# Mixture-of-experts kernel on one core: gathers signalled in halves, rows turned in the first and third round, constants' products in the turns without an expert

## What is computed

```python
def balanced_assignment(scores):
    T, E = scores.shape
    C = T // E
    taken = jnp.zeros((T,), dtype=bool)
    parts = []
    for e in range(E):
        s = jnp.where(taken, -jnp.inf, scores[:, e])
        _, idx = jax.lax.top_k(s, C)
        parts.append(idx)
        taken = taken.at[idx].set(True)
    return jnp.concatenate(parts)
...
norm = layer_norm(feat, ln_g, ln_b)
scores = jax.lax.stop_gradient(norm @ centroids.T)
sort_by_expert = balanced_assignment(scores)
routed = feat[sort_by_expert].reshape(E, C, D)
h = layer_norm(routed, ln_g, ln_b)
h = jax.nn.gelu(jnp.einsum('ecd,edf->ecf', h, w1) + b1[:, None, :])
h = jnp.einsum('ecf,efd->ecd', h, w2) + b2[:, None, :]
out = routed + h
```

## Time and profile before

| what | value |
|---|---|
| median of three runs | 1326.44 us (1326.17 to 1327.94) |
| the profiled execution's own time | 1329.28 us |
| its span in the profile | 1326.4 us |
| PE busy | 1122.2 us, 85% |
| DVE busy | 878.6 us, 66% |
| POOL busy | 775.3 us, 58% |
| ACT busy | 677.6 us, 51% |
| mean granted TensorE clock | 0.914 of full speed |

### The profile page before, as it was taken

One profiled execution on the slowest core, in us unless ns is written; L12 is line 12 of the kernel. 1 busy time (PEld: TensorE's weight loads), 2 busy tenths in 40 slices (PEclk: granted clock), 3 DMA queues, 4 the chain that ended last, 5 costly groups with the idle time before them and its releaser, 6 DMA issues. The chain is left out here.

```text
span 1326.4 us, 34010 instructions
## 1 busy us (share of the span) xinstructions
PE 1122.2 (85%) x11612; PEld 734.3 (55%) x11612; DVE 878.6 (66%) x2747; ACT 677.6 (51%) x1452; POOL 775.3 (58%) x829
## 2 busy tenths in 40 slices
PE   4999999999999996647998994869999635999996
PEld 1444444444444443434776773759998324677674
DVE  7677777777777775777788602765556768777720
ACT  3777766777776764401433453575555400343353
POOL 2878887877888785102555674645554102466675
PEclk8999999999999998856999997879999755999998
DMA  8000000000000000410221223200000410122221
GB/s 193 2 1 0 0 0 0 0 0 0 0 0 0 0 1 2 144 33 21 60 58 56 79 72 95 59 1 0 0 0 0 135 42 19 47 61 61 61 84 40
DMA packets 55851, 47.32 MB, mean 36 GB/s; under 512 B 13142, under 2 KB 47190, under 8 KB 55772
## 3 DMA queue, kind: packets, MB, share of 16 engines
q1 hardware_dynamic: 44748, 27.92, 7.6%
q0 software_dynamic: 8192, 17.84, 4.8%
q10 hardware_dynamic: 2832, 0.54, 0.3%
HBM read 28.44 MB, written 17.83 MB: 35 GB/s over the span
## 5 line engine op out<-in xcount | busy, mean ns | idle before, releaser
L349 POOL TENSOR_TENSOR patt_aa<-patt_aa,causal_aa 128x512 f32<-128x512 f32 x256 | 319.3, 1274 | 73.4 <-DVE patt_aa L528 71.5
L528 DVE TENSOR_TENSOR patt_aa<-p_second_aa,first_aa 128x512 f32<-128x512 f32 x384 | 247.5, 686 | 133.9 <-ACT first_aa L424 130.5
L424 ACT ACTIVATE first_aa<-p_first_aa 128x512 f32<-128x512 f32 x384 | 208.6, 596 | 135.9 <-PE p_first_aa L627 132.1
L627 PE MATMUL p_second_aa<-q_t_aa,k_t_aa 32*128 32x512 f32 x768 | 234.8, 641 | 0.0
L627 PE MATMUL p_first_aa<-q_t_aa,k_t_aa 32*128 32x512 f32 x768 | 217.1, 641 | 15.1 <-ACT first_aa L424 14.8
L1423 POOL DMA_INDIRECT rows_e<-norm_rows,index_e x128 | 124.5, 973 | 163.7 <-DVE index_e L1119 126.5
L646 PEld LDWEIGHTS p_z_aa<-patt_aa,v_aa 128*32 128x32 f32 x3072 | 72.2, 109 | 147.5 <-issue 79.6
L1386 ACT ACTIVATE hid_e<-p_h_e,b_e 128x512 f32<-128x512 f32 x128 | 88.6, 692 | 116.3 <-PE p_h_e L1255 116.3
L1255 PE MATMUL p_h_e<-rows_t_e,w_e 128*128 128x512 f32 x256 | 144.5, 675 | 0.1
L1340 PE MATMUL p_cnt_e<-reach_e,ones_e 128*128 128x120 bf16 x896 | 84.6, 250 | 69.7 <-DVE reach_e L1183 69.5
L1376 ACT ACTIVATE rows_t_e<-p_t_e,bias,gain 128x512 f32<-128x512 f32 x32 | 24.9, 779 | 210.7 <-PE p_t_e L1246 210.7
(11 more groups left out here) (260 smaller groups left out, 2065.4 us busy)
## 6 DMA issues: line engine op xcount, KB each, us to landing
norm_rows<-norm_n SPq DMA_DIRECT2D x32, 288.0 KB, 2.8
w_e<-L_ffn_w SPq DMA_DIRECT2D x32, 256.0 KB
x<-L_attn_a_x SPq DMA_DIRECT2D x8, 512.0 KB, 5.4
x<-ffn_rows SPq DMA_DIRECT2D x7, 512.0 KB, 6.8
rows_e<-norm_rows,index_e POOLq DMA_INDIRECT x128, 2.6
ffn_rows<-yb_e,index_e POOLq DMA_INDIRECT x64
out<-yb_e,index_e POOLq DMA_INDIRECT x64
x<-ffn_rows SPq DMA_DIRECT2D x2, 256.0 KB, 3.2
```

Source lines behind the costliest of these rows:

```text
L349: pool.tensor_tensor(patt[n % LAG][:, b, :, :], patt[n % LAG][:, b, :, :], causal[:, None, :].broadcast_to([P, 4, P]), ALU.mult).then_inc( ...
L424: act.activation(first[n % 2][:, b, :], p_first[b][:], ACT.Identity).then_inc(first_copied, 1)
L528: dve.tensor_tensor(patt[n % LAG][:, b, :, :].rearrange("p h q -> p (h q)"), p_second[(2 * n + b) % ROOMS][:], first[n % 2][:, b, :], ALU. ...
L627: pe.matmul(out[:], k_t[par][rows, half, keys * P:(keys + 1) * P], q_t[par][rows, half, :, queries * P:(queries + 1) * P], start=True, sto ...
```

## The change

It touches only `experts`, in five places.

- Each of the semaphores `gathered` becomes two, one for the gathered blocks 0 to 3 and one for 4 to 7, and `turn_rows(h)` waits for its own half only.
- TensorE's `pieces` are dealt out anew: the first turning stands in the first round behind three late downs, the second in the third round, the ups begin in the second round, and down 4 stays in its own turn.
- ScalarE copies the second half of the rows after gelu 2 and no longer ahead of gelu 0.
- VectorE's `add_back` stands at the head of window 0 (first half) and in window 2 (second half) instead of windows 2 and 4.
- In turns 0 and 1 each count is followed by three products of constants, `ones` by a 512 wide piece of `sixteenth`, into `p_h[0]`, which nobody reads.

```diff
-        gathered = [sem(f"gathered{i}_{tag}") for i in range(2)]
+        gathered = [[sem(f"gathered_{h}_{i}_{tag}") for i in range(2)] for h in range(2)]
...
                     if e >= 3:
-                        windows[2].append(lambda: add_back(e - 3, 0))
-                        windows[4].append(lambda: add_back(e - 3, 1))
+                        windows[0].insert(0, lambda: add_back(e - 3, 0))
+                        windows[2].append(lambda: add_back(e - 3, 1))
...
                     def turn_rows(h):
                         if h == 0:
-                            pe.wait_ge(gathered[par], 16 * SLOTS * half)
                             pe.wait_ge(wl[par], 48 * half)
+                        pe.wait_ge(gathered[h][par], 16 * SLOTS // 2 * half)
...
-                    late = [lambda t=t: down(t, c - 1, 1 - par) for t in range(4, SLOTS)] if rest else []
+                    late = [lambda t=t: down(t, c - 1, 1 - par) for t in range(5, SLOTS)] if rest else []
                     if compute:
-                        pieces = [late[0:2], late[2:4], turned, ups[0:1], ups[1:2], ups[2:4], ups[4:6], ups[6:8], downs[0:2], downs[2:4]]
+                        pieces = [late + turned[0:1], ups[0:2], ups[2:4] + turned[1:2], ups[4:5], ups[5:6], ups[6:7], ups[7:8] + downs[0:1],
+                                  downs[1:3], downs[3:4], downs[4:5]]
                     if isinstance(e, int) and e >= E:
-                        pieces[0:3] = [late[0:1], turned[0:1] + late[1:2], turned[1:2] + late[2:4]]
+                        pieces[0] = late[0:1] + turned[0:1] + late[1:2] + turned[1:2] + late[2:3]
+                        pieces[2] = ups[2:4]
                     if isinstance(e, int) and e == E + 1:
-                        pieces.append(downs[4:8])
+                        pieces.append(downs[5:8])
...
                         mm.then_inc(counted, 1)
+                        if not compute:
+                            for _ in range(3):
+                                pe.matmul(p_h[0][:], ones[:], sixteenth[:, 0:SLOTS, :].rearrange("p s t -> p (s t)"), start=True, stop=True)
                         for piece in pieces[n]:
                             piece()
...
-                    for h in range(2):
-                        copy_rows(h)
-                    for m in range(8):
+                    copy_rows(0)
+                    for m in range(3):
+                        gelu(m)
+                    copy_rows(1)
+                    for m in range(3, 8):
                         gelu(m)
...
                         pool.indirect_dma_start(rows[lpar][:, j, :], None, norm_rows,
-                                                bass.IndirectOffsetOnAxis(ap=list_of(l, lpar)[:, j:j + 1], axis=0)).then_inc(gathered[lpar], 16)
+                                                bass.IndirectOffsetOnAxis(ap=list_of(l, lpar)[:, j:j + 1], axis=0)).then_inc(gathered[j // 4][lpar], 16)
```

More of the change, by code:

```diff
@@ L1323, in turn @@
                                 rank_chosen(E - 1, (E - 1) % 2)
-                            if lists and n == 14:
+                            if lists and n == 13:
                                 for q in range(CHUNKS // 2):
                                     list_chunk(E - 1, q)
-                            if lists and n == 16:
+                            if lists and n == 15:
                                 list_fold(E - 1)
@@ L1334, in turn @@
                             pieces[n] = pieces[n] + [lambda q=q: list_chunk(l, q) for q in chunks]
-                        pieces[5] = pieces[5][0:1] + [lambda: list_fold(l)] + pieces[5][1:]
+                        pieces[5] = [lambda: list_fold(l)] + pieces[5]
                     for n in range(PASSES):
```

## The result

The changed kernel takes **1310.73 us** (median of 4 runs, 1309.76 to 1311.53), the kernel before 1326.62 beside it: a ratio of 0.9874, 95% interval 0.9862 to 0.9886. The forecast was 1310.6 in a range of 1304 to 1319. The profiled span is 1309.7 us, 16.7 less than before. The sum is right, but not every term of it is: one brought nothing, three others are too small, and one is a little too large.

What follows compares the result with a forecast made beforehand. Bound: the VectorE-TensorE search loop in turns 0 and 1, handovers between two nearly full engines in turns 3 to 6, products in turn 8. 1.1 + 0.6 + 1.3 + 3.7 + 1.2 = 7.9 us a layer, 15.8 off 1326.4: 1310.6, range 1304 to 1319.

Steps and rivals of the forecast that it cites:

- Turns 3 to 6, forecast 3.7: Full turns, VectorE and TensorE both nearly full: new order shortens each from 26.85 to 25.95 us, 3.7 a layer.
- the reduce comes at + 2.97: First round of a full turn: first reduce 2.97 us after turn start instead of 3.6, gain 0.6 us.
- The rival that full turns don't shorten: Turns 3 to 6: handovers of 0.1 us in each of eight rounds eat 0.8 of 0.9; 1317 us, chance 0.10.
- So the split signal is what lets the turning move: Full turns: first four gathers signalled apart land by + 2.6 us, so the first turning can stand at + 4.5.
- Its cover is 2 us: Full turns: margin between the first four gathers' landing and the first turning, put at 2 us.
- The rival that the changed order does nothing: The gathers' landing, not the order, sets the turning; time within 0.2% of before, chance 0.03.
- Turn 2, forecast 1.3: Ups begin in the second round; 24.4 us at full clock against 25.61, bounds 0 and 1.8, taken 1.3 a layer.
- TensorE waits on the gathers in the first round: Stated sign that the prediction is wrong: TensorE held by gathers in a turn's first round; no size given.
- Turns 0 and 1, forecast 1.1 + 0.6: Search turns: products of constants lift the clock, 0.28 us a round, gaining 1.1 and 0.6 us a layer.
- I take half of the most: Turns 0 and 1: clock gain at most 2.2 + 1.1 us; half of it taken, 1.1 + 0.6.
- The drain, forecast 1.2: Turns 7 to 9: 3.1 us less downs and bias left, minus copy waits of 0.9, 0.5 and 0.5; gain 1.2.
- The slower rival: Turns 0 and 1: constant products hold the counts back, 0.47 us a round if the clock never rises; 1329.6 us, chance 0.04.

Runs made afterwards that it cites:

- one_signal: Changed kernel, but the first turning waits for all eight gathers instead of its own half; 1345.51 us, 1.0146 times the kernel before.
- no_products: Changed kernel without the three products of constants in turns 0 and 1; 1316.88 us, 0.9925 of the kernel before.
- fill_tie_break: Changed kernel with more products of constants around the tie breaks of turns 0 and 1, up to turn 2's first count; 1307.18 us, 0.9851 of the kernel before.
- copies_first: Changed kernel with ScalarE making both row copies ahead of gelu 0 in turns 8 and 9 only; 1307.0 us, 0.9852 of the kernel before.
- turned_earlier: Changed kernel with both turnings moved forward by one piece of TensorE's work; 1305.45 us, 0.9841 of the kernel before.
- all_three: Changed kernel with turnings moved forward, copies ahead of the gelus in turns 8 and 9, and extra constant products around the tie break; 1304.48 us, 0.9829 of the kernel before.
- six_products: Changed kernel with six products of constants a round in turns 0 and 1 instead of three; 1312.2 us, 0.9885 of the kernel before.
- products_only: Kernel before with only the three products of constants in turns 0 and 1 added; 1322.67 us, 0.997 of the kernel before.

## Why the prediction was right, point by point

- **Turns 3 to 6, forecast 3.7, measured 4.95 and 4.62.** The mechanism held in each round: in turn 4 of layer 1 2.87, 3.38, 3.09, 2.96, 2.42, 2.10, 2.86 from reduce to reduce against 3.0, 3.4, 2.93, 3.08, 2.40, 2.12, 2.68. The turn came to 25.70 for 25.95. What was mis-sized is the first term, "the reduce comes at + 2.97" (+ 2.76), and the end, 3.26 from the eighth reduce to the next turn for 3.40. The rival that full turns don't shorten, with handovers of 0.1 in each round, is refuted: the seven rounds together came out 0.07 over the sum. Between the layers the gain differs partly by the clock before: it was 0.94 in turns 3, 4 and 5 of layer 0 and in turn 6 of layer 1 (26.96, 27.00, 26.93 and 26.89 us) and 1.00 in the four others (26.83 to 26.88), so this is worth some 0.1 a turn at most.
- **The split signal.** "So the split signal is what lets the turning move" is shown by `one_signal`: a wait of 1.81 us in the full turn 4, and 1.0146 times the kernel before. "Its cover is 2 us" was too small: it is about 3, as the gathers ended 1.2 us sooner in the turn than the rows of the kernel before had it. The rival that the changed order does nothing falls with `no_products`, which saves 9.7 us without the products.
- **Turn 2, forecast 1.3, measured -0.02 and -0.20, nothing within its spread: the step that failed.** I wrote "The same sum gives 24.4 at the full clock", gave 0 as the bound for a start at 1.2 GHz, and took a value near the other end. I should have followed TensorE through the tie break that ends turn 1: no down and no product stands in it, and the engine was busy 0.58 of 2 us. That turn 2 starts at the slow clock was in the rows: it was at 0.76 for the whole turn in the earlier trace rows. `fill_tie_break` shows the clock as the cause of 1.2 of the 1.3 and 1.5 us that were missing. What I called a sign of error, "TensorE waits on the gathers in the first round", also came, 2 times and 2.2 us in all, in the turns 2 and there alone; what is left to 24.4 in `fill_tie_break`, 0.2 to 0.35, may be that, but no run shows it.
- **Turns 0 and 1, forecast 1.1 + 0.6, measured 1.59 + 1.03.** "I take half of the most" was the mis-sized term. The most was 2.2 + 1.1, and turn 1 all but reached it. Turn 0 misses 0.6: its first 6.7 us still go at 0.50, then the clock is up until the turn's end. That is about two rounds of 0.28 that gain nothing. The Trainium skill, TensorE: Matmul & The Clock Gate, section A second HAM failure mode: psum-queue depth-cycling, says that short idles between groups of matmuls make the clock swing. The trace does not show that inside the turns: the clock rose once in turn 0 and once in turn 1, and fell only around the tie breaks that end them (0.83 and 0.85 over the turns). And a product costs 0.217 us, not the 0.31 of the bias product that I took as nearest. Part 1 of that page of the Trainium skill has 215.7 ns from start to start for 512 columns at the full clock, and the trace agrees.
- **The drain, forecast 1.2, measured 0.96 and 1.11.** The two waits are each confirmed apart. `copies_first` gets back 0.6 an expert where I had 0.5 twice. `turned_earlier` gets back 1.6 for the two waits of 0.87, one of which stood in the earlier trace rows before. Without both, in `all_three`, the rest is 3.8 and 3.9 shorter than before: the 3.1 us of downs and bias, and the 0.87 that had been there.
- **The slower rival** had the right mechanism, as `six_products` shows. But at 0.217 a product three of them fit between two counts, and in the slow rounds too they held nothing back: 2.31 and 2.37 us from reduce to reduce at the start of turn 0, where the round of the earlier trace rows and the next had 2.31 and 2.37.

That the median came within 0.2 of the forecast is luck in part. Two errors cancelled: 1.3 and more too much for turn 2, and 0.9 + 1.1 too little for turns 0, 1 and 3 to 6, in each layer. In the spans 16.7 was saved where the sum had 15.8. The rivals' times would have told me less than the turns did: the number is right, while one term of five brought nothing.

## What to carry to other kernels

Follow the clock to the place where the next heavy work begins, through the thin stretch just ahead of it: filling a search with products pays where the rounds then wait for TensorE, and leaving the thin stretch around one tie break unfilled cost 1.2 us here. When a step is moved forward, look for what its input needs: halving the signal cost nothing by itself and turned 19 us of loss into 16 of gain. A wait on one engine (0.45 us twice a turn, for a copy) is worth nothing while another sets the round, and worth its full 0.87 in the turns where it alone counts.

## What I had not expected of the hardware

The time between the two expert phases, which no edit touched, takes one of about two lengths: 261.0 to 261.7 us in seven of the traces (before, changed, `all_three`, `one_signal` and others), and 258.9 to 259.7 in four (`products_only`, `fill_tie_break`, `copies_first`, `turned_earlier`), with one at 260.8. It goes with the clock early in it. The changed kernel has

```profile
830.00:900.00 70.00, 55.25 (x293) 49.49 (x293) 45.87 (x150) 45.86 (x111) 39.08 (x69) 0.85 0.00 1
```

and `fill_tie_break`, for the same stretch,

```profile
830.00:900.00 70.00, 53.09 (x307) 47.55 (x307) 47.90 (x160) 46.73 (x116) 40.85 (x72) 0.93 0.00 1
```

The clock is higher in one than in the other, with the same program in that stretch, and the stretch between the phases is 2.4 us shorter with it (261.3 - 258.9); that the one causes the other is not shown. That is most of why `copies_first` shows 5.4 us less span than the change alone (1309.7 - 1304.3) where its two phases save 2.9. `all_three` was profiled with the longer stretch. A median of five runs of this kernel can so be off by a microsecond or two, and small edits are better read from the turns. What decides which of the two a run gets is open.
